# Spacing the scatters of routed rows over the steps of a scan and over 24 expert tiles

## The reference

```python
x = x + attn(cond(cond_1024, x))        # a gated scan over T, then attention with relative positions
x = x + ffn(cond2(x, cond_1024))        # a second scan over T, then a mixture of 8 experts, top 2
def cond2(x, h0):                       # the second scan
    xp = x @ Wx + b
    h_t = tanh(xp_t + h_{t-1} @ Wh)
def ffn(x):
    logits = x @ router_w.T
    weights, idx = top_k(softmax(logits), 2);  weights /= weights.sum() + 1e-9
    h = gelu(x @ w1[e].T + b1[e]);  out_e = h @ w2[e].T + b2[e]
    return sum over the 2 chosen experts of out_e * weight
```

## Time and profile before

| | |
|---|---|
| median of 3 runs | 749.21 us (748.86 to 749.55) |
| the profiled execution's own time | 753.76 us |
| its span, first to last instruction | 751.4 us |
| TensorE products (PE) busy | 589.5 us, 78% |
| VectorE (DVE) busy | 433.5 us, 58% |
| GpSimd (POOL) busy | 400.2 us, 53% |
| ScalarE (ACT) busy | 393.1 us, 52% |
| mean granted TensorE clock | 0.909 |
| second scan, first to last tanh | 426.4 to 572.6 us |
| scatters of chunks 0 to 6 | 448.1 to 580.1 us |
| scatters of the 71 tiles | 590.2 to 740.5 us |

### The profile page before, as it was taken

One profiled execution on the slowest core, in us unless ns is written; L12 is line 12 of the kernel. 1 busy time (PEld: TensorE's weight loads), 2 busy tenths in 40 slices (PEclk: granted clock), 3 DMA queues, 4 the chain that ended last, 5 costly groups with the idle time before them and its releaser, 6 DMA issues. The chain is left out here.

```text
span 751.4 us, 27301 instructions
## 1 busy us (share of the span) xinstructions
PE 589.5 (78%) x10479; PEld 445.0 (59%) x10479; DVE 433.5 (58%) x2041; ACT 393.1 (52%) x1112; POOL 400.2 (53%) x433
## 2 busy tenths in 40 slices
PE   2888888888889999999988675444445977999993
PEld 1565565555667677677757332222222977999993
DVE  1666666666578677787763244334444653456775
ACT  4666666666226555555545232222222755899893
POOL 3455445445168789877784213344444365566552
PEclk9999999999999999999999876666675888999997
DMA  7265555555787577766660232230021123225453
GB/s 244 114 233 219 198 217 198 206 202 207 257 232 203 162 202 202 196 171 175 196 226 3 101 127 90 93 93 30 30 51 38 33 72 78 59 70 154 148 154 101
DMA packets 111940, 108.66 MB, mean 145 GB/s; under 512 B 7136, under 2 KB 85472, under 8 KB 111440
## 3 DMA queue, kind: packets, MB, share of 16 engines
q1 hardware_dynamic: 107120, 97.66, 41.1%
q0 software_dynamic: 4320, 8.89, 3.4%
q10 hardware_dynamic: 384, 0.52, 0.2%
HBM read 59.43 MB, written 45.52 MB: 140 GB/s over the span
## 5 line engine op out<-in xcount | busy, mean ns | idle before, releaser
L515 POOL TENSOR_TENSOR sc<-sc,mx 128x1024 f32<-128x1024 f32 x64 | 121.2, 1899 | 51.0 <-DVE mx L673 51.0
L406 POOL TENSOR_SCALAR QD<-q_all,mask 128x128 f32<-128x128 f32 x126 | 88.8, 717 | 98.6 <-DVE pre L361 95.6
L673 DVE CUSTOM_DVE_ANT_0 sc<-banks,s2t 128x128 f32<-128x128 f32 x512 | 112.1, 286 | 47.5 <-PE banks L566 45.2
L1180 POOL DMA_INDIRECT expert_outputs<-yr,xr x71 | 79.2, 1115 | 71.1 <-issue 37.0
L1172 POOL DMA_INDIRECT expert_inputs<-rows,slotu x56 | 54.5, 973 | 93.4 <-DVE slotu L1333 78.5
L731 ACT ACTIVATE PT<-banks 128x512 f32<-128x512 f32 x128 | 69.8, 596 | 63.1 <-PE banks L579 63.1
L1108 ACT ACTIVATE h<-banks,bias 128x32 f32<-128x32 f32 x128 | 36.8, 288 | 111.2 <-PE banks L420 56.7
L420 PE MATMUL banks<-h,wh 128*32 128x32 f32 x1016 | 38.3, 227 | 70.9 <-ACT h L1108 39.4
L1126 ACT ACTIVATE hid<-banks,w1b 128x128 f32<-128x128 f32 x284 | 81.1, 368 | 21.9 <-PE banks L1069 10.9
L420 PEld LDWEIGHTS banks<-h,wh 128*32 128x32 f32 x1016 | 22.7, 123 | 108.6 <-ACT h L1108 74.0
L352 DVE COPY s2stage<-banks 128x512 f32<-128x512 f32 (+1 forms) x90 | 76.6, 852 | 16.5 <-PE banks L253 16.5
(11 more groups left out here) (145 smaller groups left out, 1054.7 us busy)
## 6 DMA issues: line engine op xcount, KB each, us to landing
s_scratch<-s2stage SPq DMA_DIRECT2D x32, 1024.0 KB, 4.8
s2t<-s_scratch SPq DMA_DIRECT2D x64, 512.0 KB, 4.9
xr<-expert_inputs SPq DMA_DIRECT2D x71, 64.5 KB
xz<-in_xz SPq DMA_DIRECT2D x8, 512.0 KB, 5.9
yb<-expert_outputs SPq DMA_DIRECT2D x16, 256.0 KB
w2all<-in_w2b SPq DMA_DIRECT2D x8, 320.0 KB
w1a<-in_w1b SPq DMA_DIRECT2D x8, 258.0 KB
k_all<-in_xT SPq DMA_DIRECT2D x1, 2048.0 KB, 10.0
```

The source lines that it names most:

```text
L406: op = pool.tensor_scalar(QD[G % 3][:, :, h, :], q_all[:, :, quad(G)].rearrange("p b t -> p t b"), mask[:, h:h + 1], None, ALU.mult)
L515: pool.tensor_tensor(sc[U % RING][:], sc[U % RING][:], mx[U % RING][:].unsqueeze(2).broadcast_to([P, HH, T]), ALU.subtract)\
L673: op = dve.tensor_tensor_reduce(out=sc[r][:, h, :], in0=ps[2 * (U % 2) + h // 4][:, h % 4 * T:(h % 4 + 1) * T], in1=s2t[r][:, h, :], scale ...
L1180: pool.indirect_dma_start(yg_dram, bass.IndirectOffsetOnAxis(xr[k][:, D:].bitcast(U32), 0), yr[k][:], None).then_inc(s_ys[k], 16)
```

## The change

In the scan, the eight scatters of chunk c no longer follow each other at once: the k-th waits until step (c + 1) · 16 + 14 + 2k of the scan can begin (`s_h2` starts at 1 and counts one for each tanh). Those whose step would be past the end, seven of chunk 6, go to the expert tiles: one each behind the scatters of tiles 0 to 6. Chunk 7's eight go behind tiles 8, 9, 11, 12, 14, 15, 17 and 18. Because these numbers need tiles that are written out, 24 tiles are written out instead of 16 on every engine, and the hardware loop has five turns instead of six; ScalarE's wait for the late table stays ahead of tile 16.

```diff
+        UNROLLED = SPREAD + RX
+
         def over_tiles(eng, step, late=None):
-            for i in range(SPREAD // RX):
+            for i in range(UNROLLED // RX):
+                if late and i == SPREAD // RX:
+                    late()
                 for k in range(RX):
                     step(i, k, i * RX + k, True, True)
-            if late:
-                late()
-            with eng.Fori(SPREAD // RX, NS // RX) as i:
+            with eng.Fori(UNROLLED // RX, NS // RX) as i:
...
+        def scatter_step(c, k):
+
+            return (c + 1) * TC + 14 + 2 * k
+
+        behind_scan = [(NCH - 2, k) for k in range(2 * JT) if scatter_step(NCH - 2, k) >= T]
+        scatter_tiles = dict(enumerate(behind_scan))
+        scatter_tiles.update((RX + k + k // 2, (NCH - 1, k)) for k in range(2 * JT))
+        assert len(behind_scan) < RX and scatter_step(NCH - 3, 2 * JT - 1) < T
...
-                    c, o = m - 1, 1 - m % 2
+                    c = m - 1
                     pool.wait_ge(s_slot, c + 2)
                     for k in range(2 * JT):
-                        pool.indirect_dma_start(xg_dram, bass.IndirectOffsetOnAxis(slotu[o][:, k:k + 1], 0),
-                                                rows[o][:, k, :], None).then_inc(s_sc[o], 16)
+                        if scatter_step(c, k) < T:
+                            pool.wait_ge(s_h2, scatter_step(c, k) + 1)
+                            scatter(c, k)
+
+                def scatter(c, k):
+                    o = c % 2
+                    pool.indirect_dma_start(xg_dram, bass.IndirectOffsetOnAxis(slotu[o][:, k:k + 1], 0),
+                                            rows[o][:, k, :], None).then_inc(s_sc[o], 16)
...
-                    if isinstance(s, int) and RX <= s < RX + 2 * JT:
-                        if s == RX:
+                    if isinstance(s, int) and s in scatter_tiles:
+                        c, n = scatter_tiles[s]
+                        if (c, n) == (NCH - 1, 0):
                             pool.wait_ge(s_slot, NCH + 1)
-                        pool.indirect_dma_start(xg_dram, bass.IndirectOffsetOnAxis(slotu[1][:, k:k + 1], 0),
-                                                rows[1][:, k, :], None).then_inc(s_sc[1], 16)
+                        scatter(c, n)
```

## The result

The changed kernel takes 725.67 us (median of 4 runs, 722.54 to 728.83), the kernel before 749.22 beside it (4 runs, 748.86 to 749.55): ratio 0.9686, 95% interval 0.9653 to 0.9719. The forecast was 731, range 692 to 757. The profiled execution took 725.47 us with a span of 722.8, for 753.76 and 751.4 before.

What follows compares the result with a forecast made beforehand. Scatter bursts stopping the second scan's product-tanh chain were taken to bound the kernel. Terms: -21 scan, +3 clock, -8 behind the scan, +8 tiles, sum -18 us, from 749.2 to 731; range 692 to 757.

Steps and rivals of the forecast that it cites:

- What bounds the kernel: Second scan: bursts of eight back-to-back GpSimd scatters stop the product-tanh chain, 9.2 us each, six bursts, 55 us.
- Spread in the scan: Scan: 49 spaced scatters at 0.7 us each cost 34 us, so -21; a lower clock adds +3.
- Behind the scan: Last tanh to first tile transpose: seven scatters leave the way of 64 small products, -8 us.
- In the tiles: Expert tiles: fifteen double tiles cost 22.4 us where eight cost 14.6, so +8, bounds -2 to +13.
- tiles 0 to 6 are back to back: 7 × 1.83 = 12.8: Expert tiles: each of the first seven double tiles costs 1.83 us, the loss per second scatter read before the change.
- 8 us are spare and 4 to 5 go: nothing: SyncE's load of tile 24 waits for tile 18's second scatter, two tiles later, but its lead hides this.
- a tile 24 that waits for its rows: Expert tiles: listed among the signs that would show the forecast wrong.
- the other signs: Scatters about 2.1 us apart, alternate tanhs 0.4 to 1.0 late, no wait over 2, first transpose within 3, tiles 0 to 6 at 2.5 to 3.5.
- Code: Eight more tiles written out on each engine, one loop turn less: nothing, bound ±2 us.
- Rival 1: Scan: a lone scatter is free there too, -55 in the scan, 694 us; chance 0.25.
- Rival 2: Scan: a lone scatter costs 1.26 us, 764 us; slower than before from 1.07 us each; chance 0.23.
- Rival 3: Scan: bursts only coincide with the stops, time unchanged at 749 us; chance 0.05.

Runs made afterwards that it cites:

- the probes: Changed kernel plus six single GpSimd operations (two scatters, two plain DMA writes, two memsets) and SyncE writes early in the scan; 728.0 us, one execution.
- the second batch: Changed kernel again (726.62 us, ratio 0.9706), the better order and the probes, on a chip where the kernel before took 748.95 us.
- the row of eight: Changed kernel with chunk 6's left-over scatters ahead of tile 0 (three) and beside tiles 1, 2, 4, 5; chunk 7's eight beside tiles 8 to 15; 678.23 us, 1.0006.
- the better order: Changed kernel with three of chunk 6's seven left-over scatters ahead of tile 0 and four beside tiles 1, 2, 4 and 5; 723.44 us, ratio 0.9660.
- code-alone run: Kernel before with 24 tiles written out in place of 16, scatters untouched; 677.87 us, ratio 0.9996 to the kernel before.

## Why the prediction was right, and where it wasn't

*What bounds the kernel*: right on the chip it was read from. The bursts cost 55 of the 56 us of stops by the step count, 54 to 55 against an even chip's scan; I had 55. (TensorE's digits in the scan go down to 4, not to 3 as I wrote.)

*Spread in the scan*, forecast -21 of stops and +3 of clock: it was -27 and +2.4 (127 steps at the clock's two levels, stops taken out, 90.4 us before and 92.8 after). The term that was mis-sized is the price of a scatter, 0.55 us in the mean for the 0.7 taken, inside the bounds of 0.4 and 1.0; the probes gave 0.34 and 0.43. 49 × 0.15 is the 7 us between -18 and -25.1.

*Behind the scan*, forecast -8: it was -8.3, 2.8 us from the last tanh to the first transpose.

*In the tiles*, forecast +8: +5.4. That more doubled tiles stop TensorE more fits the trace; the sizes were wrong. By the forecast's own measure, the starts of GpSimd's scatters, tiles 0 to 8 take 25.8 us where they took 16.8: +9.0. The mis-sized step is "tiles 0 to 6 are back to back: 7 × 1.83 = 12.8"; they cost 1.29 each. Tiles 8 to 20 take 34.1 for 37.4, that is 11.3 above the even pace where I had 9.6. Nor is 1.83 a price that each double pays: before the change tile 15 comes 8.4 us behind tile 14 and tile 22 comes 10.6 behind tile 20, and these two places hold 13.3 of the 15.7 us lost up to tile 24. "8 us are spare and 4 to 5 go: nothing" was off too: the load went 1.8 us ahead of its transpose for 7.7 before, so 5.9 went, and tile 24 came 1.2 us late. I had named a tile 24 that waits for its rows as a sign of being wrong, and it shows, if small; the other signs came as forecast (tiles 0 to 6 at 3.4 us each on GpSimd, no wait of the tanh over 2 us within the scan).

The 4 to 5 us that the same order costs on even chips, for which the forecast had no term, come with longer waits for loads, not with stops. On the stopping chip the loss stands ahead of that load, so the two figures being alike is no proof of one cause. How much of the +5.4 is lag and how much stops was not measured apart.

*Code*: nothing, as said; 0.9996 for it alone.

*The rivals*. Rival 1 (a lone scatter is free in the scan) fell on the stopping chips and holds on the even ones, but so does a free burst there. Rival 2 fell: 0.55, far from its 1.07. Rival 3, that bursts only coincide, fell on the stopping chips: the stops moved with the scatters, both in the changed kernel and at the probes. The Trainium skill (SBUF — State Buffer, "Who interferes with whom") says that TensorE and ScalarE wait on nobody and that a DMA never contends with a compute engine. That fits the even chips' scans (steps of 0.68 us across a burst) and not the stopping ones' (9.2 us lost to a burst); whether the stop arises at a port, of which that section speaks, no run here shows. I had given 0.05 to "unchanged"; on the two even chips where the scan part ran alone that is what it gives (0.9987 and 0.9973). I had no case for a price that depends on the chip.

**What stays open**: why some chips stop and others don't. The first comparison and the second batch stopped (the record doesn't say whether both ran on one chip); three other chips, in three batches, were even. The same kernel issues the same scatters at the same lengths. No run tells whether it is the chip itself, a setting of it, or what else went on beside it. Whether the pause between scatters or only their number sets the price on a stopping chip is only suggested by the kernel's own bursts and lone scatters (1.15 and 0.50 each) and by the pair above (0.83 each); the runs made to test it met even chips. The parts of the change were never run by themselves on a stopping chip either, so that they add up there rests on the stretches of the whole kernel. Nor was the row of eight measured on a stopping chip, where it may or may not keep the better order's 3 us.

## What to carry to other kernels

Price a change that moves DMA issues on more than one chip before keeping it: this one was worth 3.1% and 2.9% where bursts stop the scan, and kernels with its tile order cost 0.8% on one even chip and 0.7% and 0.9% on another, with other spacings in the scan. The order with three scatters ahead of tile 0, four beside tiles 1, 2, 4 and 5 and the rest in a row takes that loss away on even chips; it is the version that I would keep, after a run on a stopping one. And when a queue falls behind, look for what waits for its last entry: on the even chips, moving work to "free" places of GpSimd cost nothing (tile 16 stood level) until the load behind the last scatter ran out of its lead.

## What the runs showed of the hardware

- The same kernel took 748.95 and 749.22 us in two comparisons and 677.4 to 678.9 on three other chips. The part ahead of the scan is the same on both kinds (425.8 to 428.7 us to the first tanh on the one, 424.5 to 429.2 on the other). All of the 76.6 us between the spans of the kernel before (751.4) and of the code-alone run (674.8) lie where GpSimd scatters: 54 us in the scan, 8.5 behind it, 14 in the tiles. Of the 14, 12 stand ahead of tile 24, where some tiles have two scatters; tiles 24 to 44, with one each, take 37.9 us on the one and 38.0 on the other, so not every scatter on a stopping chip costs time.
- On a stopping chip the price of a scatter hangs on its company: 0.34 and 0.43 us at the start of the scan, 0.50 in the mean of lone ones, 0.83 in a pair, 1.15 in bursts. Nearly all of it lies between the recorded end of a product and the engine that waits for it.
- One late step is the same on both kinds of chip and has nothing to do with scatters: step 1 of round 2, 2.20 us in the changed kernel and 2.71 in the code-alone run, whose timeline shows why. The product of the attention's output projection stands ahead of the step's own:

```profile
448.78 0.29 ACT L1110 ACTIVATE h<-banks,bias 128x32 f32<-128x32 f32 x1 [0.39 <-PE banks L420]
...
449.91 0.69 DVE L1209 TENSOR_TENSOR x1r<-banks,x1r 128x512 f32<-128x512 f32 x1
...
450.66 0.66 PE L420 MATMUL banks<-wo,q_all 128*32 128x128 f32 x8 [1.95 <-DVE x1r L1209]
...
451.08 0.34 PE L420 MATMUL banks<-h,wh 128*32 128x32 f32 x8
...
451.49 0.29 ACT L1110 ACTIVATE h<-banks,bias 128x32 f32<-128x32 f32 x1 [2.42 <-PE banks L420]
```

  TensorE's queue holds a side product ahead of the step's product, and that one waits for VectorE to empty its bank. It costs 1.5 to 2 us once; a side product placed later might save it, which wasn't tried. I had put all of the first burst's loss down to scatters.
